# A four-stage graph-attention, expert and state-space kernel: the first attention's product made channel-major, its row sums computed ahead of it, three smaller edits, and a new hand-written order

## The reference, cut to what matters

```python
# stage A (layer 0, graph net)
o1  = relu(xn @ mlp1_w + b)                # 256 x 512
h   = o1 @ W_fc                            # first attention, no mask
e   = leaky_relu(f1[:, None] + f2[None, :], 0.2)
hp  = elu(softmax(e) @ h);  o = elu(hp) + o1
o2  = relu(o @ mlp2_w + b)                 # 256 x 256
y   = masked attention of o2 with W_hand;  x = x + relu(elu(elu(y)) + o2)
# stage Q (layer 0, routed expert): the 127 rows with the largest weight of each
#   batch (ties by position) pass a 256->1024->256 gelu net, scaled by the weight
# stage G (layer 1, graph net): one masked attention, 256 channels
# stage M (layer 1, state space): 256 -> z (512), xBC (640), dt (8); causal
#   convolution of 4 taps, silu, one chunk of 256 with
#   Y = (C B^T * decay) @ (x dt) + D x, gate, RMS norm, 512 -> 256
```

## Time and profile before

| | |
|---|---|
| median of 3 runs | 3889.12 us (3888.59 to 3889.54) |
| the profiled execution | 3887.89 us, of which its span is 3886.2 us |
| PE busy | 3668.9 us, 94% |
| PEld, DVE busy | 3171.3 us (82%), 3107.9 us (80%) |
| ACT, POOL busy | 2355.4 us (61%), 1002.1 us (26%) |
| mean granted TensorE clock | 0.982 |
| chain that ended last | PE 68%, DVE 22%, ACT 5%, issue 4% |

### The profile page before, as it was taken

How to read it: one execution, slowest core, us unless ns; L and a number is a source line. 1 busy time by engine, 2 the same in 40 slices (tenths; PEclk the granted TensorE clock), 3 DMA queues, 4 the chain that set the end, 5 groups by cost and what they waited for, 6 DMA issues and landing times.

```text
span 3886.2 us, 64302 instructions
## 1 busy us (share of the span) xinstructions
PE 3668.9 (94%) x21016; PEld 3171.3 (82%) x21016; DVE 3107.9 (80%) x8243; ACT 2355.4 (61%) x5250; POOL 1002.1 (26%) x1817
## 2 busy tenths in 40 slices
...
GB/s 92 11 23 28 30 38 27 30 38 33 24 38 38 27 30 38 27 30 38 32 25 38 38 27 30 38 27 30 38 31 26 38 38 27 30 38 27 30 28 30
DMA packets 73763, 126.85 MB, mean 33 GB/s; under 512 B 9984, under 2 KB 64128, under 8 KB 65536
## 3 DMA queue, kind: packets, MB, share of 16 engines
...
...
## 4 chain that ended last, share of the span: by engine, by line
PE 68%; DVE 22%; ACT 5%; issue 4%; DVEq 0%; POOL 0%; DMA 0%; POOLq 0%
PE A L1179 12%; PE M L1315 7%; PE A L1199 6%; PE A L1217 6%; PE Q L1303 6%; PE M L1349 6%; PE A L1264 3%; DVE yss L1109 3%; PE A L1226 3%; PE Q L1226 3%; PE Q L1264 3%; DVE u L875 3%; DVE ga_ L1003 2%; PE A L1209 2%; DVE acc L1050 2%
## 5 line engine op out<-in xcount | busy, mean ns | idle before, releaser
L1179 PE MATMUL A<-w_fc,o1T 128*128 128x256 f32 (+1 forms) x2048 | 460.9, 383 | 3.7 <-ACT o1T L619 3.7
L1179 PEld LDWEIGHTS A<-w_fc,o1T 128*128 128x128 f32 x2048 | 382.5, 189 | 65.0 <-ACT o1T L619 5.3
L535 POOL TENSOR_TENSOR var_m<-mv_m,epsilon 128x2 f32<-128x2 f32 x64 | 12.5, 195 | 1414.5 <-DVE mv_m L818 1414.5
L786 ACT ACTIVATE dec<-cumB,cumcol 128x256 f32<-128x256 f32 (+1 forms) x1024 | 366.3, 443 | 0.0
L1041 DVE SCALAR_TENSOR_TENSOR acc<-M,w_conv,acc 128x255 f32<-128x255 f32 (+2 forms) x768 | 315.0, 470 | 0.0
L1315 PE MATMUL M<-xT_m,w_in 128*128 128x256 f32 x1280 | 297.5, 379 | 0.9 <-DVE tz L1083 0.8
L1199 PE MATMUL A<-h,low 128*128 128x257 f32 (+1 forms) x1024 | 256.6, 395 | 22.5 <-DVE low L859 14.0
L1315 PEld LDWEIGHTS M<-xT_m,w_in 128*128 128x128 f32 x1280 | 237.8, 190 | 32.2 <-DVE tz L1083 2.1
L1296 PE MATMUL Q<-selT,w_up 128*128 128x128 f32 x2048 | 249.5, 275 | 0.9 <-ACT selT L722 0.9
L1217 PE MATMUL A<-e,w_mlp 128*128 128x256 f32 x1024 | 242.8, 391 | 1.5 <-DVE e L883 1.5
L1303 PE MATMUL Q<-w_down,gsq 128*128 128x256 f32 x1024 | 237.0, 385 | 7.1 <-DVE gsq L1014 7.1
...
## 6 DMA issues: line engine op xcount, KB each, us to landing
cumB<-cum_dram SPq DMA_DIRECT2D x64, 1024.0 KB, 4.7
...
w_up<-in_L_ffn_w SPq DMA_DIRECT2D x1, 1024.0 KB, 10.1
w_down<-in_L_ffn_w SPq DMA_DIRECT2D x1, 1024.0 KB, 11.3
```

The lines of the kernel that those rows point to most:

```text
L786: last = nc.scalar.activation(dec[:, h, :], columns[:, h, :], ACT.Relu, bias=cumcol[:, i, h:h + 1], scale=-1.0)
L1179: last = nc.tensor.matmul(rows1(half, u, 2), o1T[:, k, u * P:(u + 1) * P], w_fc[:, k, half, 0:D + 2 * i], start=(k == 0), stop=(k == KH - 1))
```

## The change

What it does, part by part:

1. **Row sums ahead.** VectorE's `a_maxima` makes four more small results; ScalarE (`a_sums`) makes the same factors as a row and the second operand; VectorE (`a_sums`) adds up max(...) with an accumulator and takes one reciprocal; TensorE's new step `a_spread` (two transposes into A0) brings it into row form; VectorE's `a_spread` multiplies `fac` with it, and only then ScalarE's `a_low` and VectorE's `a_probs` follow. The attention weights are thus normalised before the product.
2. **Channel-major product.** `a_att` has `h1` as stationary and `p1` as moving operand, 256 columns wide, in the same number of matmuls. `a_uturn` falls away on TensorE and VectorE; the exponentials and maxima run on 512 columns at a time, in two halves.
3. **Banks.** Both halves of `a_mlp1` go into A1, one after the other, with ScalarE's evacuation between; `a_fc`, `b_res`, `b_pturn`, `b_att` and `a_turn` exchange their banks accordingly.
4. **Rank in one pass**: one instruction for each row tile in place of two, the column form of the weights by ScalarE in place of `q_route_col`.
5. **B C^T at full height**: `bT`, `cT` have 128 partitions, the upper 64 zero.
6. **`m_sq`**: two additions in place of the strided reduction.
7. **New order** on all five engines, with TensorE's largest lag 6 in place of 5 (70 turns, 58 of them full), and SyncE's load, residual, spread and store in another order with other lags.

The diff, cut to its core:

```diff
@@ STEPS
     "tensor": [
+        ("q_ffn1.1", 4), ("m_xrow", 6), ("b_pturn", 2), ("m_cum_col", 6), ("b_att", 2), ("b_res", 2), ("m_cb", 6),
+        ("q_ffn2", 4), ("q_scatter", 4), ("a_fc.0", 1), ("m_y.0", 6), ("m_y.1", 6), ("a_fc.1", 1), ("g_turn", 4),
+        ("m_turn", 5), ("a_bcast", 1), ("g_proj", 4), ("m_out", 6), ("m_ss", 6), ("a_spread", 1), ("g_bcast", 4),
+        ("m_dt", 5), ("m_z", 5), ("q_route", 3), ("a_att.0", 1), ("a_att.1", 1), ("m_xbc_a", 5), ("m_xbc_b", 5),
+        ("q_gather", 3), ("g_pturn", 4), ("m_da", 5), ("a_mlp2", 1), ("g_att", 4), ("a_turn", 0), ("b_proj", 1),
+        ("a_mlp1.0", 0), ("b_bcast", 1), ("q_ffn1.0", 3), ("a_mlp1.1", 0),
     "vector": [
+        ("m_cb", 7), ("q_norm", 4), ("m_norm", 6), ("a_stats", 0), ("q_scatter", 5), ("m_mix.0", 7), ("q_x2", 5),
+        ("m_mix.1", 7), ("g_stats", 5), ("b_elu_c", 3), ("b_x1", 3), ("g_norm", 5), ("a_fc", 2), ("m_y.0", 7),
+        ("a_fcol", 2), ("m_y.1", 7), ("q_route", 4), ("a_maxima", 2), ("g_proj", 5), ("m_sq", 7), ("a_sums", 2),
+        ("m_ms", 7), ("a_spread", 2), ("g_mask", 5), ("m_out", 7), ("g_lrelu", 5), ("m_dt", 6), ("g_max", 5),
+        ("a_probs", 2), ("m_gate", 6), ("q_rank", 4), ("g_pturn", 5), ("a_elu_c", 2), ("q_stats", 3),
+        ("m_conv_b.0", 6), ("m_conv_b.1", 6), ("m_scan", 6), ("m_conv_b.2", 6), ("b_proj", 2), ("a_norm", 0),
+        ("g_elu_b", 5), ("b_mask", 2), ("m_silu", 6), ("b_lrelu", 2), ("b_max", 2), ("q_gelu_a", 4), ("g_x3", 5),
+        ("q_gelu_b", 4), ("m_cum_col", 6), ("b_pturn", 2), ("m_stats", 5), ("q_ffn2", 4),
     "scalar": [
+        ("g_elu", 5), ("g_att", 5), ("b_proj", 2), ("m_silu", 6), ("a_mlp1", 1), ("b_exp", 2), ("q_gelu_a", 4),
+        ("b_pturn", 2), ("m_xrow", 6), ("q_gelu_c", 4), ("m_decay.0", 6), ("m_decay.1", 6), ("b_att", 2),
+        ("b_elu_b", 2), ("g_turn", 4), ("a_fcol", 1), ("m_turn", 5), ("m_gated", 6), ("a_sums", 1), ("a_factors", 1),
+        ("g_proj", 4), ("a_low", 1), ("m_dt_exp", 5), ("m_z", 5), ("q_route", 3), ("g_exp", 4), ("a_att", 1),
+        ("a_elu_b", 1), ("m_xbc_a", 5), ("m_xbc_b", 5), ("q_gather", 3), ("g_pturn", 4), ("a_mlp2", 1), ("a_turn", 0),
     "gpsimd": [
+        ("m_turn", 7), ("m_norm", 6), ("m_xrow", 7), ("q_turn", 4), ("g_norm", 5), ("m_rms", 7), ("m_dt_log", 6),
+        ("m_da", 6), ("q_norm", 3), ("a_norm", 0),
     "sync": [
-        ("a_load", 0), ("a_residual", 2), ("m_store", 6), ("m_spread", 5),
+        ("m_store", 9), ("m_spread", 8), ("a_residual", 3), ("a_load", 0),
@@ ScalarE
+            def a_sums(b):
+                act.wait_ge(S["gcol_ready"], b)
+                for i, rate in enumerate((1.0, ALPHA)):
+                    last = nc.scalar.activation(brow[:, i, :], A1[:, N:2 * N], ACT.Exp, bias=falls[:, i:i + 1], scale=rate)
+                last.then_inc(S["brow_ready"], 1)
+                act.wait_ge(S["ends_ready"], nth(b, 2, 2))
+                nc.scalar.activation(ends[:], ends[:], ACT.Exp).then_inc(S["ends_exp"], 1)
...
+                for u in range(U):
+                    last = nc.scalar.activation(low[:, u, :], brow[:, 1, :], ACT.Copy, scale=ends[:, 1, u:u + 1])
+                last.then_inc(S["part_ready"], 1)
@@ VectorE
+            def a_sums(b):
+                v.wait_ge(S["part_ready"], b)
+                for u in range(U):
+                    last = nc.vector.scalar_tensor_tensor(out=low[:, u, :], in0=brow[:, 0, :], scalar=ends[:, 0, u:u + 1],
+                                                          in1=low[:, u, :], op0=ALU.mult, op1=ALU.max,
+                                                          accum_out=rs1[:, u:u + 1])
...
+                nc.vector.reciprocal(r1[:], rs1[:]).then_inc(S["r1_ready"], 1)
+            def a_spread(b):
+                v.wait_ge(S["rb_ps"], b)
+                v.wait_ge(S["fac_ready"], b)
+                nc.vector.tensor_tensor(fac[:], fac[:], A0[:, None, 0:N].to_broadcast([P, 2, N]), ALU.mult)\
+                    .then_inc(S["norm_ready"], 1)
...
-                    last = nc.vector.scalar_tensor_tensor(out=junk[:, u * P:(u + 1) * P], in0=wrow[:, u * P:(u + 1) * P],
-                                                          scalar=1.0, in1=ident[:], op0=ALU.mult, op1=ALU.mult,
-                                                          accum_out=wcol[:, u:u + 1])
...
+                    last = nc.vector.scalar_tensor_tensor(out=spare[:, u, :], in0=wrow[:], scalar=wcol[:, u:u + 1],
+                                                          in1=tie_gap[:, u, :], op0=ALU.subtract, op1=ALU.is_ge,
+                                                          accum_out=rank[:, u:u + 1])
...
-                nc.vector.tensor_reduce(yss[:], ysq.rearrange("p k n -> p n k"), AX_X, ALU.add)\
-                    .then_inc(S["yss_ready"], 1)
+                nc.vector.tensor_tensor(ysq[:, 0:2, :], ysq[:, 0:2, :], ysq[:, 2:4, :], ALU.add).then_inc(S["sq_half"], 1)
+                v.wait_ge(S["sq_half"], b)
+                nc.vector.tensor_tensor(yss[:], ysq[:, 0, :], ysq[:, 1, :], ALU.add).then_inc(S["yss_ready"], 1)
@@ TensorE
+                for c in range(2):
                     for j in range(U):
-                        last = nc.tensor.matmul(rows1(half, u, 1), p1[:, j, u * P:(u + 1) * P],
-                                                h1[:, j, half, 0:D + 1 - half],
+                        last = nc.tensor.matmul((A0, A2)[half][:, c * N:(c + 1) * N], h1[:, j, half, c * P:(c + 1) * P],
+                                                p1[:, j, :], start=(j == 0), stop=(j == U - 1))
-            def a_uturn(b):
...
```

More of the change, by code:

```diff
@@ L17 @@
 NEG = 9.0e15
+LEAST = 2.0 ** -126
 GELU_CUBE = 0.044715
@@ L29 @@
     "tensor": [
[L30 to L34, removed]
@@ L166, in gnn_ffn_mamba_kernel @@
         gcol = sb("gcol", [P, U])
+        tcol = sb("tcol", [P, U])
+        tops = sb("tops", [P, 2])
+        falls = sb("falls", [P, 2])
+        ends = sb("ends", [P, 2, U])
+        brow = sb("brow", [P, 2, N])
         bcol = sb("bcol", [P, U])
@@ L715, in q_route @@
                 act.wait_ge(S["w_ps"], b)
+                before(act, S["x2_ready"], b)
+                nc.scalar.activation(wcol[:], wsum[:], ACT.Identity, bias=c_route[:, 0:1])
                 nc.scalar.activation(wrow[:], Q0[:, 0:N], ACT.Identity, bias=c_route[:, 0:1])\
@@ new lines, in a_sums @@
+                nc.vector.reciprocal(r1[:], rs1[:]).then_inc(S["r1_ready"], 1)
[4 more added lines that the diff above has]
+                    .then_inc(S["norm_ready"], 1)
+            def a_elu_c(b):
+                for i, ps in enumerate((A0, A2)):
+                    v.wait_ge(S["e1x_ready"], nth(b, 2, i + 1))
+                    half = e1[:, 2 * i:2 * i + 2, :]
+                    nc.vector.tensor_tensor(half, two(ps), half, ALU.max).then_inc(S["u1_ready"], 1)
+                for i in range(2):
+                    v.wait_ge(S["u1_ready"], nth(b, 2, i + 1))
+                    half = e1[:, 2 * i:2 * i + 2, :]
+                    nc.vector.scalar_tensor_tensor(out=half, in0=half, scalar=-1.0, in1=o1T[:, 2 * i:2 * i + 2, :],
+                                                   op0=ALU.add, op1=ALU.add).then_inc(S["z1_ready"], 1)
```

211 lines of the change are left out of this document (92 added, 119 removed).

## The result

| | before | after |
|---|---|---|
| median | 3888.91 us (3888.59 to 3889.54) | 3946.52 us (3943.22 to 3948.78) |
| the profiled execution, its span | 3887.89, 3886.2 us | 3948.06, 3946.3 us |
| ratio to before | | 1.0147, 95% interval 1.013 to 1.0165 |

The change makes the kernel 1.5% slower, where 0.9% faster was forecast: 3946.5 against 3854 us, outside the range.

What follows compares the result with a forecast made beforehand. TensorE was taken as the bound: a turn of 54.66 + 1.20 + 0.10 + 0.67 = 56.6 us, and 568.2 for head and tail + 58 x 56.6 = 3851 us of span, so 3854 us; range 3812 to 3900.

Steps and rivals of the forecast that it cites:

- what is late next: TensorE's new order checked step by step against what it waits for; adds 1.20, 0.10 and 0.67 us a turn.
- A turn without waits: TensorE's turn of 57.16 us, less 2.72 for removed steps and waits, plus 0.22 for a_spread: 54.66 us.
- (a): Gelu chain ahead of q_ffn2: TensorE waits 1.20 us in all, about 1.0 before b_att, plus 0.10 cold start.
- (b): q_scatter directly behind q_ffn2: TensorE waits for VectorE's yff, +0.67 us.
- (c): m_y.0 behind a_fc.0: VectorE's second m_mix ends at 15.94, TensorE gets there at 16.1; just covered.
- (d): New row-sum chain to a_spread and a_att: covered, 0.3 us spare; without m_z as cover it would cost 3.
- (e): Elu after the product: hidden, ready 1.1 us ahead of a_mlp2; a_mlp1's single bank is covered by q_ffn1.0.
- Filling and draining: Head 311 us and tail 257.5, together 568 in place of 513.7, with one full turn less; bounds -15 and +12.
- SyncE's case: Rival: SyncE's spread starts late behind store and load; three us later gives T 58.2, 3946 us; 9%.
- The clock's: Rival: the clock falls at (a), about 4 us of matmuls take double, T near 60, 4050 us; 5%.
- More near misses: Rival: (c), (d) and the place at b_proj have under 0.6 us spare; +0.6 gives T 57.2, 3886 us; 16%.

Runs made afterwards that it cites:

- the undisturbed kernel: The kernel after with GpSimd's xdt cut to 8 columns, x3b and xs to 16, the rest of the tiles constant: 3903.19 us, ratio 1.0036.
- The three small edits: The kernel before, old order, plus m_sq as two additions, the one-pass rank and B C^T at full height: 3823.82 us, ratio 0.9835.

## Why the prediction was wrong

**The step that failed** is "what is late next": it checked each step of TensorE against chains whose durations came from the old order's rows, and took these to hold in the new one. `xn_q` at 0.73 a pair and `sc_b` at 0.69 [before's group means above] were the durations beside which GpSimd did nothing large. In the new order a pair of `xn_q` took up to 2.40 and `sc_b` 1.43 in the mean. Without the collisions 0.82 us of each of 58 turns went away: 48 of the 95 us. This step alone doesn't explain the miss. With the collisions gone the kernel takes 3903 us, still slower than before and just outside the range. The other half are terms that were too small: 24 us of costs of steps in the full turns, and 23 us of filling and draining.

- **A turn without waits (54.66).** Right in kind: `a_uturn` is gone, `m_cb` to the end of its pair is at its pace, `m_xrow` costs 0.87 in the undisturbed kernel. B C^T was mis-sized, 0.20 for 0.39 (measured in the old order), outside its own bound of 0.3; this error would have made the kernel faster than forecast.
- **(a) and (b).** Without collisions the frame fits: `q_ffn2` stands at 1985.23 - 1977.75 (start of `q_ffn1.1`) = 7.48 against 7.42, `q_scatter` at 11.71 against 7.42 + 3.55 + 0.67 = 11.64. From start to start (a) costs 0.98 ahead of `b_att` and 0.27 ahead of `q_ffn2`, 1.25 where 1.30 was forecast, and (b) costs 0.78 for 0.67. With collisions, in the turn shown, (b) is 0.53 more, and `b_pturn`, which was no place in the prediction, 0.42; the mean over the turns is 0.82 for both.
- **(c).** `m_y` stood just covered, at 16.23 (forecast 16.1), with `m_mix.1` ended 0.2 before; true, but a start of GpSimd's `xs` 0.02 us ahead of `m_mix.1` makes it late.
- **(d), (e).** Covered in the full turns, as said; neither `a_spread` nor `a_att` waits there. The order that moved VectorE's steps took that cover away.
- **The remaining 0.4 us of a turn** (57.02 against 56.6; 24 us in all) has no wait of its own. Step by step from start to start, against what the 54.66 holds for each: `m_y` takes 2.75, not 2.65; the two halves of `a_fc` on its sides 7.13, not 7.04; `g_proj` 1.82, not 1.74; (a) and (b) 0.06 more. That is 0.33; the rest is hundredths in other steps. The first half of `a_fc`, 16 records of 256 columns, takes 3.55 where `q_ffn2`'s took 3.45, the same 0.1 as beside the half-height product. Whether `m_y`'s narrower form is the cause was not tried.
- **Filling and draining: 23 us.** Predicted turns of the filling 43, 45, 45.5, 49.5, 53 (236.0 in all; the prediction adds 236.3); read 44.4, 47.7, 47.3, 55.2, 54.8. In them the row-sum chain is bare: in the fourth TensorE waits 2.18 for `r`, 1.74 for `low` and 3.22 for `e`, where steps that stand between them in a full turn are missing. From the first `a_mlp1` to the first `m_xrow` the kernel after takes 256.7 and the one with the three cuts 254.9, so it is hardly the collisions. The turns of the draining, forecast as 52.8, 47.5, 47, 45.5 and 40.5, come to 240.2, 6.9 more. At the end, the last batch needs 28.2 us from `m_xrow` against a forecast of 24.2: ScalarE's decay matrices have moved behind `m_xrow` and `m_cum_col`. PE's timeline of the last `m_y` after, and then before:

```profile
3930.70 5.33 PE L1420 MATMUL M<-dec,xdt 128*64 128x256 f32 x32 [8.31 <-DVE dec L1115]
```

```profile
3870.41 5.39 PE L1392 MATMUL M<-dec,xdt 128*64 128x256 f32 x32 [6.10 <-POOL xdt L592]
```

  It starts 12.6 after the last `m_xrow` (3918.09), where it was 9.6 (3860.77). The cost of filling and draining is read from traces alone; no run took it apart.
- **The rivals.** SyncE's case named 3946 us, which is the time measured, but by coincidence: its mechanism is false, `cumB` is never late. SyncE's order cost 0.4 us a turn by another way, through the store and `x3b`. The clock's is false for this kernel. "More near misses" is the family to which the truth belongs, with a cause of which the prediction didn't speak; its price of 0.6 us (3886 us) and its 16% were too little.

**Where the gain of the whole change went.** The three small edits alone are worth 1.02 us of a turn. The kernel after contains them, and with its collisions cut it has a turn of 57.02, 0.88 longer than theirs. The channel-major product and the new order, taken together, therefore cost 0.9 us a turn before any collision: they remove `a_uturn`'s 0.93 and the waits at `m_xrow` and `a_att`, some 1.8 in all from start to start, and pay with 0.82 and 0.52 of idle time at the front, two more transposes and the tails and restarts around them, some 2.6. The product and the order weren't tried apart. Then come 0.82 for the collisions. Against before, a turn is 57.84 - 57.16 = 0.68 longer, 39 us over 58 turns; head and tail are 29 and 49 us longer with one full turn of 57 less, 21 us; together the 60 us by which the span grew.
